# Attention stage of a fused layer: the row maxima transposed between the second gate and up products, and the residual rows' statistics given places of their own behind row maxima

## The chip, the cores and the metric

The kernel runs on one core of a Trainium2 chip. Its time is that of one execution of the whole program on the device, in microseconds (us); lower is better. The engines are TensorE (PE, with its weight loads as PEld), VectorE (DVE), ScalarE (ACT), GpSimd (POOL) and SyncE (SP), which here only issues transfers. Each works through its own list of instructions in order and waits on semaphores.

## The reference

The input x has 16 sequences of 512 rows of 256 numbers. Cut to its frame, with the two branches named:

```python
x = L0_attn_x                       # (16, 512, 256)
xn = _layernorm(x, axis=-1)
x = x + _L0_attn_ref(xn, ...) + _L0_ffn_ref(xn, ...)
# _L0_attn_ref: a state-space block (convolution, softplus, scan over 512 steps)
# _L0_ffn_ref:
y = mla(rmsnorm(xn, w_ln1), ...)    # 16 heads, causal softmax, latent keys and values
x = xn + y
x = x + moe(rmsnorm(x, w_ln2), ...) # a shared expert, and 2 of 7 experts chosen per row
```

## The kernel before

Three stages follow one another: the attention stage (`build_attn`), a stage for the chosen experts, and the state-space stage. The change is in the first alone.

The attention stage is a software pipeline over the 16 sequences. One **round** works on several sequences at once: on an older one it finishes the output projection, the second norm, the routing and the shared expert; on the next one the second pass of scores, the softmax and the values; on a younger one the first pass of scores, from which only the row maxima are kept; and on the youngest the projections. What stands where in a round is written by hand. The second pass of scores gives 64 numbered places; the table `AT` hangs every other item on a place, as (place, kind, i, j). `ORDER` is the list that results, and **every engine walks the same list** and does its own part of each item, so the table sets the order on all five engines together.

The items that matter here, with the lines of the kernel before:

- `wo` (PE L924): the output projection, four items at places 25, 27, 29 and 31. With every second one DVE adds the residual rows (L697, `f_xn<-f_Z,f_xn`), and in the kernel before also takes the statistics of those rows (L701 and L705). With the last one POOL makes from the statistics the scale of the second norm (L520 to L523) and then the sum `xs` (L526), which releases the semaphore `xs_ready`.
- `s1`: the first pass of scores (PE L840, hidden part L857, bank pair `f_Y`) and its row maxima (DVE L632). An item with j below 2 fills both banks of `f_Y`, and the next one can only start when these are read.
- `xrload`, `keep`, `stack`, `so`, `sl`: transfers on SP's queue, in this order. `xrload` (L364) waits for `xs_ready`. `keep` (L377) stores the parts of keys and queries, the six `stack` items (L387, two transfers each) read them back, `so` (L395) stores the sums of the softmax after the third `stack` item, and `sl` (L398) reads them back behind the sixth.
- `rp` (DVE L680), at place 48: the reciprocal of these sums. Behind it on DVE stand the first up product's multiplication (`u`, L770), the splitting of the maxima into three parts (`nm`, L684 to L692), the routing (`rank`, 16 small operations, L724 to L742) and the second gate product's multiplication (`g`, L766), and then the second up product's (L770).
- `nmt` (PE L903): the transposition of the split maxima, which ACT copies and SP puts beside the queries for the next round's second pass. `pfx` (PE L951, L953): the prefix sums for the routing.
- `g` and `u` (PE L960): the gate and up products of the shared expert, two each.

All of these but `s1` and the second pass share one pair of banks, `f_Z`, which are filled in turn. A product can start only when the one two before it in this ring has been read:

```python
    def freed(k, r):
        i, n = place(k, r)
        return ring_free[ring_of(k)][i], n
```

In the kernel before the order in the ring is gate 1, up 1, gate 2, up 2, `nmt`, `pfx`. So `nmt` goes into the bank of gate 2.

Of the kernel before, what the change touches and what calls it, by code (L numbers as in the profile page):

```python
# [16 lines left out]
def build_attn(nc, ctx, x_tm, out_tm, info_dram, run_dram, stat_dram, hs, w_ln1, w_ln2, W_kvd, W_qd, W_ka, W_kra, W_krb, W_qa, W_qb, W_vu, W_o,  # L17
# [7 lines left out]
    TT = SEQ // P  # L25
# [10 lines left out]
    def sb(name, shape, dt=f32):  # L36
        return ctx.enter_context(nc.sbuf_tensor(name, shape, dt))
# [38 lines left out]
    xn = sb("f_xn", [P, TT, DM])  # L76
# [15 lines left out]
    nm = sb("f_nm", [P, TT, NH])  # L92
# [8 lines left out]
    h2 = sb("f_h2", [P, TT, DM])  # L101
# [4 lines left out]
    lg = sb("f_lg", [P, TT, ER])  # L106
# [4 lines left out]
    rank = sb("f_rank", [P, TT, ER])  # L111
# [24 lines left out]
    for q in range(NG * TT):  # L136
        g, kb = divmod(q, TT)
# [7 lines left out]
    STAGE = {kind: 2 for kind in ("bnc", "h1", "h1a", "T", "lat", "kq", "split", "mid", "keep", "stack")}  # L145
    STAGE.update({kind: 1 for kind in ("stack1", "s1", "nm", "nmt", "v")})
    STAGE.update({kind: 0 for kind in ("mvx", "mvs", "xrload", "xn", "s2", "pv", "oc", "so", "sl", "rp", "ro", "rl", "ym")})
    STAGE.update({kind: -1 for kind in ("sl1", "rp1", "ro1", "rl1", "ym1", "wo", "h2", "h2a", "ht", "route", "lg", "rank", "pfx", "g", "u", "d")})
    STAGE.update({"scat": -2, "d": -2, "xload": 3, "bn": 3})
    S1 = [("s1", i, n) for i in range(NH // 2) for n in range(3)]  # L150
    AT = {}
    for n, kind, i, j in ((0, "mvx", 0, 0), (0, "bnc", 0, 0), (0, "sl1", 1, 0), (1, "stack1", 1, 0), (2, "stack1", 1, 1), (3, "stack1", 1, 2), (5, "stack1", 1, 3), (6, "stack1", 1, 4), (8, "stack1", 1, 5), (3, "d", 0, 0), (3, "h1", 0, 0), (4, "mvs", 0, 0), (5, "d", 1, 0), (5, "h1a", 0, 0),
# [4 lines left out]
                          (36, "stack", 0, 0), (37, "stack", 0, 1), (39, "stack", 0, 2), (40, "stack", 0, 3), (42, "stack", 0, 4), (43, "stack", 0, 5), (38, "ht", 0, 0), (39, "ht", 1, 0), (42, "route", 0, 0), (43, "route", 1, 0), (44, "lg", 0, 0),  # L157
                          (46, "g", 0, 0), (48, "xn", 0, 0), (49, "u", 0, 0), (50, "nm", 0, 0), (52, "rank", 0, 0), (52, "g", 1, 0), (55, "u", 1, 0),
                          (56, "nmt", 0, 0), (58, "pfx", 0, 0), (59, "bn", 0, 0)):
        AT.setdefault(n, []).append((kind, i, j))  # L160
    for n, item in enumerate(S1):
        AT.setdefault(2 + n * 47 // len(S1), []).append(item)
# [18 lines left out]
    def ring_of(k):  # L181
        return {"s2": "X", "s1": "Y"}.get(k[0], "Z")
# [16 lines left out]
    def place(k, r):  # L199

        ring = ring_of(k)
        n = index(r)
        if isinstance(n, int):
            n = sum(len(NUMBERS[m, ring]) for m in range(FIRST, n)) + NUMBERS[n, ring][k]
            return n % 2, n // 2
        first = sum(len(NUMBERS[m, ring]) for m in range(FIRST, FULL))
        n = first + (r[1] - FULL) * len(NUMBERS[FULL, ring]) + NUMBERS[FULL, ring][k]
        return n % 2, r[0] * len(NUMBERS[FULL, ring]) + n // 2
# [72 lines left out]
    def used(k, r):  # L281

        i, n = place(k, r)
        return ring_free[ring_of(k)][i], n + 1
# [4 lines left out]
    def free_sem(k, r):  # L289
        return ring_free[ring_of(k)][place(k, r)[0]]  # L290
# [136 lines left out]
    def _(pool):  # L427
# [32 lines left out]
        def chain(s, K, b, n, ins):  # L460
            ins.then_inc(s, 1)
            pool.wait_ge(s, K * b + n)

        def do(kind, i, j, b, r):
# [23 lines left out]
            if kind == "kq" and i == 1 and j % 2 == 1:  # L488
                g, n = i, j // 2
# [5 lines left out]
            if kind == "split":  # L495
                g = i
# [9 lines left out]
            if kind == "mid":  # L506
                g = i
# [5 lines left out]
            if kind in ("ym", "ym1"):  # L513
                pool.wait_ge(shares_loaded, 16 * (PAIRS * b + i + 1))
                yT = yT_[:, parity(kind, r), :, :]
                tt(yT[:, 2 * i:2 * i + 2, :], yT[:, 2 * i:2 * i + 2, :], shares[:, :, :], ALU.mult).then_inc(y_done, 1)  # L516
            if kind == "wo" and i == TT - 1:

                pool.wait_ge(stats2_done, TT * (b + 1))
                chain(sc2_step, 4, b, 1, tt(sc2[:, 0, :], mv2[:, :, 0], mv2[:, :, 0], ALU.mult))  # L520
                chain(sc2_step, 4, b, 2, tt(sc2[:, 1, :], sc2[:, 0, :], mv2[:, :, 1], ALU.add))
                chain(sc2_step, 4, b, 3, tt(sc2[:, 2, :], sc2[:, 1, :], consts[:, 1, :], ALU.pow))
                tt(sc2[:, 3, :], sc2[:, 2, :], consts[:, 2, :], ALU.add).then_inc(sc2_step, 1)  # L523
                pool.wait_ge(xr_loaded, 16 * (b + 1))
                pool.wait_ge(ot_stored, 16 * b)
                tt(xs[:, :, :], x2[:, :, :], xr[:, :, :], ALU.add).then_inc(xs_ready, 1)  # L526
            if kind == "scat":
# [4 lines left out]
                for t in range(2 * i, 2 * i + 2):  # L532
                    for k in range(TOPK):
                        pool.indirect_dma_start(hs, bass.IndirectOffsetOnAxis(ap=info_i[:, t, k:k + 1], axis=0),
                                                h2[:, t, :], None).then_inc(scattered, 16)
        run(nc.gpsimd, do)
        pool.wait_ge(scattered, 16 * TT * TOPK * BATCH)

# [86 lines left out]
    def _(dve):  # L625
        def full(k, r):
            dve.wait_ge(*filled(k, r))
            return bank_of(k, r)

        def do(kind, i, j, b, r):  # L630
# [23 lines left out]
            if kind == "kq" and i == 1:  # L654
                n = j // 2
# [37 lines left out]
            if kind == "wo" and i % 2 == 1:  # L693
                n = i // 2
                if n == 0:
                    dve.wait_ge(xn_done, 2 * b + 2)
                dve.tensor_tensor(x2[:, 2 * n:2 * n + 2, :], full(("wo", n), r)[:, :].rearrange("p (j d) -> p j d", j=2),  # L697
                                  xn[:, 2 * n:2 * n + 2, :], ALU.add).then_inc(free_sem(("wo", n), r), 1)
                for t in range(2 * n, 2 * n + 2):
                    dve.wait_ge(*used(("wo", n), r))  # L700
                    dve.bn_stats(st2[:, t, :], x2[:, t, :]).then_inc(stat2, 1)  # L701
                for t in range(2 * n, 2 * n + 2):
                    dve.wait_ge(stat2, TT * b + t + 1)
                    dve.sem_inc(taken)
                    dve.bn_aggr(mv2[:, t, :], st2[:, t, :]).then_inc(stats2_done, 1)  # L705
# [65 lines left out]
            if kind == "d":  # L771
                bank = full(("d", i), r)
                dve.wait_ge(xs_ready, b + 1)
                dve.scalar_tensor_tensor(xs[:, 2 * i:2 * i + 2, :], bank[:, :].rearrange("p (j d) -> p j d", j=2), 0.5,
                                         xs[:, 2 * i:2 * i + 2, :], ALU.mult, ALU.add).then_inc(free_sem(("d", i), r), 1)
        run(nc.vector, do)

    @block.tensor
# [1291 lines left out]
```

## Time and profile before

| | |
|---|---|
| time, median of 3 runs | 4051.83 us (4046.68 to 4064.09) |
| the profiled execution | 4053.83 us, its span 4052.0 us |
| PE busy | 88% of the span |
| DVE, ACT, POOL busy | 71%, 62%, 53% |
| attention rounds with everything in them | 78 to 85 us each, from 160 to 1290 us |
| mean granted clock of TensorE | 0.949 of full speed |

The profile is of one execution. Its timeline gives, for each engine, the start and the duration of an instruction or of a run of like ones, and in brackets how long the engine had stood idle before it and what ended that. A place in a round is found by its operation and tile: the residual addition, for instance, is the DVE row L697.

### The profile page before, as it was taken

The numbers are of one execution on the slowest core, as the hardware profiler recorded it, in microseconds if no ns is written. First come the engines' busy times: TensorE is split into PE (matmuls) and PEld (weight loads), VectorE is DVE, ScalarE is ACT, GpSimd is POOL, SyncE is SP. The second block draws the span as 40 slices with busy tenths as digits, with TensorE's granted clock in tenths as the row PEclk, the third lists the DMA queues.
The fourth block names the chain that finished last, engine by engine and source line by source line (L and its number), as shares of the span: only waits on it lengthen the run. The fifth ranks groups of instructions, "written<-read, shape, count | busy, mean of one in ns | idle before, by whom it ended". The sixth has DMA issues, their size and how long they took to land.

```text
span 4052.0 us, 70010 instructions
## 1 busy us (share of the span) xinstructions
PE 3579.4 (88%) x22072; PEld 2713.9 (67%) x22072; DVE 2892.4 (71%) x5392; ACT 2521.9 (62%) x6537; POOL 2154.4 (53%) x1083
## 2 busy tenths in 40 slices
PE   4899999999998759998799999998999999999887
PEld 1354445445554447777588888888887888888776
DVE  3455655555554222222799999999999999999997
ACT  2545555455454213332788878788887878888783
POOL 3243344334332200000578787787878778787774
PEclk7899999999999779999899999999999999999998
DMA  4333333333332167665222222121222212222221
GB/s 112 97 93 114 101 117 98 110 106 112 94 111 74 34 182 211 208 210 176 87 73 103 84 81 99 65 99 71 104 84 81 98 66 99 71 104 84 81 80 40
DMA packets 286364, 416.64 MB, mean 103 GB/s; under 512 B 78261, under 2 KB 250678, under 8 KB 263672
## 3 DMA queue, kind: packets, MB, share of 16 engines
q1 hardware_dynamic: 273048, 380.79, 29.6%
q0 software_dynamic: 12288, 33.57, 2.3%
q8 instruction: 102, 1.67, 0.2%
q10 hardware_dynamic: 864, 0.10, 0.1%
q14 instruction: 62, 0.51, 0.0%
HBM read 330.30 MB, written 83.17 MB: 102 GB/s over the span
## 4 chain that ended last, share of the span: by engine, by line
DVE 36%; issue 11%; PE 2%; POOL 1%; DVEq 1%; ACT 1%; DMA 0%; SPq 0%; POOLq 0%; ACTq 0%
DVE m_S L1774 8%; DVE m_PR L1774 8%; DVE m_S L1766 8%; DVE m_PR L1766 8%; DVE m_ub L1751 2%; DVE m_yz L1785 1%; DVE m_x L1735 1%; POOL m_ub L1554 1%; DVEq L1765 1%; DVE m_th_x L1743 1%; ACT m_dA L1663 1%; PE m_F L1884 0%; PE m_Y L1922 0%; PE m_F L1858 0%; PE m_F L1934 0%
## 5 line engine op out<-in xcount | busy, mean ns | idle before, releaser
L1554 POOL TENSOR_TENSOR m_ub<-m_Bb,m_dtx 128x2048 f32<-128x2048 f32 x254 | 1157.0, 4567 | 280.6 <-PE m_Y L1922 176.1
L1663 ACT ACTIVATE m_dA<-m_dt,m_a_neg 128x128 f32<-128x128 f32 x4096 | 1211.1, 388 | 129.6 <-DVE m_S L1774 129.2
L1922 PE MATMUL m_Y<-m_ub,m_ident 128*128 128x128 f32 x8192 | 956.2, 278 | 62.7 <-DVE m_ub L1751 62.4
L1922 PEld LDWEIGHTS m_Y<-m_ub,m_ident 128*128 128x128 f32 x8192 | 939.5, 194 | 73.8 <-DVE m_ub L1751 73.5
L632 DVE TENSOR_REDUCE f_nm<-f_Y 128x1 f32<-128x512 f32 (+3 forms) x896 | 432.4, 531 | 308.9 <-PE f_Y L857 306.8
L552 ACT ACTIVATE f_pt<-f_X 128x512 f32<-128x512 f32 (+1 forms) x704 | 372.5, 556 | 406.8 <-PE f_X L857 403.5
L1766 DVE SCALAR_TENSOR_TENSOR m_PR<-m_dA,m_S 128x512 f32<-128x512 f32 x512 | 355.8, 695 | 26.1 <-POOL m_ub L1554 7.5
L1766 DVE SCALAR_TENSOR_TENSOR m_S<-m_dA,m_PR 128x512 f32<-128x512 f32 x512 | 354.8, 693 | 12.0
L1774 DVE CUSTOM_DVE_ANT_1 m_S<-m_S,m_ub 128x512 f32<-128x512 f32 x512 | 353.2, 690 | 0.8 <-issue 0.8
L1774 DVE CUSTOM_DVE_ANT_1 m_PR<-m_PR,m_ub 128x512 f32<-128x512 f32 x512 | 353.2, 690 | 0.2 <-DVE m_PR L1766 0.2
L1751 DVE TENSOR_TENSOR m_ub<-m_S,m_Cb 128x512 f32<-128x512 f32 x512 | 349.5, 683 | 0.0
L1751 DVE TENSOR_TENSOR m_ub<-m_PR,m_Cb 128x512 f32<-128x512 f32 x512 | 349.3, 682 | 0.0
L516 POOL TENSOR_TENSOR f_yT<-f_yT,f_shares 128x1024 f32<-128x1024 f32 x32 | 75.3, 2353 | 462.3 <-DMA f_shares<-f_shares_dram 462.3
L1884 PE MATMUL m_F<-m_xpad,m_cv_diag 128*128 128x256 f32 x1024 | 285.6, 427 | 0.0
L840 PE MATMUL f_Y<-f_kst,f_qst 96*128 96x512 bf16 (+3 forms) x1024 | 236.8, 316 | 52.0 <-DVE f_nm L632 27.6
L1200 DVE SCALAR_TENSOR_TENSOR e_sg<-e_th,e_G 128x512 f32<-128x512 f32 x70 | 48.1, 687 | 324.7 <-ACT e_th L1144 324.7
L846 PE MATMUL f_X<-f_qst,f_kst 99*128 99x512 bf16 (+3 forms) x1024 | 253.6, 317 | 27.3 <-ACT f_pt L552 19.2
L1505 POOL MEMSET m_ident<- 128x128 f32 x1 | 0.2, 205 | 470.2 <-POOLq L2047 470.2
L1884 PEld LDWEIGHTS m_F<-m_xpad,m_cv_diag 128*128 128x128 f32 x1024 | 201.5, 207 | 71.4 <-issue 45.2
L1858 PE MATMUL m_F<-m_xnT,m_w_in 128*128 128x256 f32 x1024 | 236.0, 384 | 2.6 <-DMA m_w_in<-L_attn_W_in 1.6
L840 PEld LDWEIGHTS f_Y<-f_kst,f_qst 96*128 96x128 bf16 x1024 | 88.3, 102 | 186.2 <-issue 87.3
L1858 PEld LDWEIGHTS m_F<-m_xnT,m_w_in 128*128 128x128 f32 x1024 | 193.1, 193 | 28.1 <-DMA m_w_in<-L_attn_W_in 2.0
(233 smaller groups left out, 6009.6 us busy)
## 6 DMA issues: line engine op xcount, KB each, us to landing
m_Bb<-m_bc_dram SPq DMA_DIRECT2D x64, 1024.0 KB, 4.7
m_Cb<-m_bc_dram SPq DMA_DIRECT2D x64, 1024.0 KB, 6.3
f_parts_dram<-f_parts SPq DMA_DIRECT2D x32, 768.0 KB, 4.1
f_kst<-f_parts_dram SPq DMA_DIRECT2D x192, 128.0 KB, 2.6
f_qst<-f_parts_dram SPq DMA_DIRECT2D x192, 128.0 KB, 2.6
e_rows<-sorted_rows SPq DMA_DIRECT2D x70, 256.0 KB, 2.8
e_wg<-Wg SPq DMA_DIRECT2D x70, 256.0 KB, 2.9
e_wu<-Wu SPq DMA_DIRECT2D x70, 256.0 KB, 4.0
```

Source lines behind the costliest of these rows:

```text
L552: act.activation(out, cols(bank_of(k, r)), func, **kw).then_inc(free_sem(k, r), 1)
L632: ins = dve.tensor_reduce(out, cols(full(k, r)), AX.X, ALU.max, negate=True)
L840: pe.matmul(bank[:, c0:c0 + n], qst[p][0:KS, h, qb * P:(qb + 1) * P], kst[p][0:KS, h, 0:n], start=(c0 == 0), stop=False, skip_group_check= ...
L846: pe.matmul(bank[:, c0:c0 + n], kst[p][:, h, kb * P:(kb + 1) * P], qst[p][:, h, kb * P:SEQ], start=(c0 == 0), stop=False, skip_group_check ...
L1554: pool.tensor_tensor(ub[:, h, i, :, :], Bb[:, s, :, :], dtx[:, m, None, s * SN:(s + 1) * SN].to_broadcast([P, NST, SN]), ALU.mult).then_in ...
L1663: last = act.activation(dA[:, h, i, n, :], dtt[:, par, m, s * SN:(s + 1) * SN], ACT.Exp, scale=a_neg[:, m, n:n + 1])
L1751: return dve.tensor_tensor(ub[:, h, 1:3, :, cols], state[:, :].rearrange("p (i n b) -> p i n b", i=2, n=NST), Cb[:, s, None, :, cols].to_b ...
L1766: dve.scalar_tensor_tensor(new, dA[:, h, :, :, cols].rearrange("p i n b -> p (i n) b"), DA_MIN, old, ALU.max, ALU.mult).then_inc(p_step, 1)
L1774: dve._custom_dve(bass.dve_ops.TENSOR_ADD_SAT, out=new, in0=new, in1=ub[:, h, 0:2, :, cols].rearrange("p i n b -> p (i n) b"), s0=CLIP, s1 ...
L1858: last = pe.matmul(F[(1 + i) % 4][:, m, :], w_in[:, k, blk * P:(blk + 1) * P], xnT[:, k, :], start=(k == 0), stop=(k == KM - 1))
L1884: last = pe.matmul(F[1 + i][:, j, :], cv_diag[:, k * MI + m, :], xpad[:, m, k * BATCH:k * BATCH + CN], start=False, stop=(k == TAPS - 1))
L1922: last = pe.matmul(Y[:, i * SN:(i + 1) * SN], ident[:, :], ub[:, h, 1 + i, n, :], start=False, stop=(n == NST - 1), skip_group_check=True)
```

## The change

Two things are moved. First, the statistics of the residual rows become an item of their own, `x2s`, at places 28 and 32, one place behind the residual addition, and POOL's chain on them goes with the second one. The reciprocal and the scaling of the second norm (`h2`, `h2a`) move one place down. Second, `nmt` moves from place 56 to 54, the second up product from 55 to 57, and `pfx` from 58 to 59. No instruction is added or taken away.

```diff
@@ -145,7 +145,7 @@
-    STAGE.update({kind: -1 for kind in (..., "wo", "h2", ...)})
+    STAGE.update({kind: -1 for kind in (..., "wo", "x2s", "h2", ...)})
...
@@ -153,10 +153,10 @@
-                          (29, "wo", 2, 0), (30, "mid", 1, 0), (31, "wo", 3, 0), (33, "xrload", 0, 0), (34, "keep", 1, 0), (34, "h2", 0, 0), (35, "h2a", 0, 0),
+                          (28, "x2s", 0, 0), (29, "wo", 2, 0), (30, "mid", 1, 0), (31, "wo", 3, 0), (32, "x2s", 1, 0), (33, "xrload", 0, 0), (34, "keep", 1, 0), (35, "h2", 0, 0), (36, "h2a", 0, 0),
...
-                          (46, "g", 0, 0), (48, "xn", 0, 0), (49, "u", 0, 0), (50, "nm", 0, 0), (52, "rank", 0, 0), (52, "g", 1, 0), (55, "u", 1, 0),
-                          (56, "nmt", 0, 0), (58, "pfx", 0, 0), (59, "bn", 0, 0)):
+                          (46, "g", 0, 0), (48, "xn", 0, 0), (49, "u", 0, 0), (50, "nm", 0, 0), (52, "rank", 0, 0), (52, "g", 1, 0),
+                          (54, "nmt", 0, 0), (57, "u", 1, 0), (59, "pfx", 0, 0), (59, "bn", 0, 0)):
@@ -514,7 +514,7 @@
-            if kind == "wo" and i == TT - 1:
+            if kind == "x2s" and i == 1:
 
                 pool.wait_ge(stats2_done, TT * (b + 1))
@@ -696,6 +696,8 @@
                 dve.tensor_tensor(x2[:, 2 * n:2 * n + 2, :], full(("wo", n), r)[:, :].rearrange("p (j d) -> p j d", j=2),
                                   xn[:, 2 * n:2 * n + 2, :], ALU.add).then_inc(free_sem(("wo", n), r), 1)
+            if kind == "x2s":
+                n = i
                 for t in range(2 * n, 2 * n + 2):
                     dve.wait_ge(*used(("wo", n), r))
                     dve.bn_stats(st2[:, t, :], x2[:, t, :]).then_inc(stat2, 1)
```

From L698 on, a line of the kernel before has a number higher by two in the changed one.

**DVE, at the second pair of residual rows.** `f_xn<-f_Z,f_xn` is the residual addition, `f_st` and `f_mv` are the statistics, `f_nm<-f_Y` are row maxima, three operations for one head of `s1`. Before:

```order
L697 TENSOR_TENSOR f_xn<-f_Z,f_xn 128x512
L701 BN_STATS f_st<-f_xn 128x6 x2
L705 BN_AGGR f_mv<-f_st 128x2 x2
L632 TENSOR_REDUCE f_nm<-f_Y 128x1 x6
L708 RECIPROCAL f_sc<-f_sc 128x4
L632 TENSOR_REDUCE f_nm<-f_Y 128x2
```

The changed kernel, at the same place:

```order
L697 TENSOR_TENSOR f_xn<-f_Z,f_xn 128x512
L632 TENSOR_REDUCE f_nm<-f_Y 128x1 x3
L703 BN_STATS f_st<-f_xn 128x6 x2
L707 BN_AGGR f_mv<-f_st 128x2 x2
L632 TENSOR_REDUCE f_nm<-f_Y 128x1 x3
L710 RECIPROCAL f_sc<-f_sc 128x4
L632 TENSOR_REDUCE f_nm<-f_Y 128x2
```

Three row maxima of one head now stand ahead of the statistics.

**PE, at the second gate and up products.** `f_Z<-f_h2T,f_wg` is a gate product, `f_Z<-f_h2T,f_wu` an up product, `f_Z<-f_identb,f_nm_part` is `nmt`, `f_X` is the second pass of scores, `f_O` the values, and `f_Z<-f_chosen,f_tri` the start of `pfx`. The list is read from the second gate product on; what only repeats is left to the rows shown. Before:

```order
L873 MATMUL f_O<-f_pt,f_va 32x512 x4
L784 REGISTER_ALU
L960 MATMUL f_Z<-f_h2T,f_wu 128x512 x2
L846 MATMUL f_X<-f_qst,f_kst 128x384
L857 MATMUL f_X<-f_mask_k,f_identb 128x128
L900 REGISTER_ALU
L903 MATMUL f_Z<-f_identb,f_nm_part 48x128 x4
L784 REGISTER_ALU
L846 MATMUL f_X<-f_qst,f_kst 128x384
L857 MATMUL f_X<-f_mask_k,f_identb 128x128
L846 MATMUL f_X<-f_qst,f_kst 128x256 x2
```

The changed kernel, at the same place:

```order
L875 MATMUL f_O<-f_pt,f_va 32x512 x4
L786 REGISTER_ALU
L902 REGISTER_ALU
L905 MATMUL f_Z<-f_identb,f_nm_part 48x128 x4
L848 MATMUL f_X<-f_qst,f_kst 128x384
L859 MATMUL f_X<-f_mask_k,f_identb 128x128
L786 REGISTER_ALU
L848 MATMUL f_X<-f_qst,f_kst 128x384
L859 MATMUL f_X<-f_mask_k,f_identb 128x128
L962 MATMUL f_Z<-f_h2T,f_wu 128x512 x2
L848 MATMUL f_X<-f_qst,f_kst 128x256 x2
```

`nmt` and the second up product have changed places around two items of the second pass. In the ring of banks the order becomes gate 1, up 1, gate 2, `nmt`, up 2, `pfx`: `nmt` goes into the bank of up 1, and up 2 into that of gate 2.

## Rows read from the trace of the kernel before

**Rows 1.** The page: busy time of TensorE and its share of the span.

```profile
PE 3579.4 (88%) x22072; PEld 2713.9 (67%) x22072; DVE 2892.4 (71%) x5392; ACT 2521.9 (62%) x6537; POOL 2154.4 (53%) x1083
```

**Rows 2.** Waits, 170 to 1300 us: total us, times, longest.

```profile
DVE f_sums L680 <- DMA f_sums<-f_sums_dram: 38.1, 13, 5.0
...
PE f_Z L903 <- DVE f_sg L766: 32.3, 14, 4.0
```

**Rows 3.** Timeline (start, us, operation), PE: second up product, `nmt`; last row another round.

```profile
565.11 1.99 PE L960 MATMUL f_Z<-f_h2T,f_wu 128*128 128x512 f32 x4
566.93 0.33 PE L846 MATMUL f_X<-f_qst,f_kst 99*128 99x384 bf16 x1
...
570.75 0.38 PE L903 MATMUL f_Z<-f_identb,f_nm_part 128*48 128x128 bf16 x4 [3.44 <-DVE f_sg L766]
...
974.08 0.38 PE L903 MATMUL f_Z<-f_identb,f_nm_part 128*48 128x128 bf16 x4 [0.74 <-DVE f_sg L766]
```

**Rows 4.** Timeline, DVE, from the reciprocal of the sums to the second gate.

```profile
563.50 0.35 DVE L680 RECIPROCAL f_sums<-f_sums 128x32 f32<-128x32 f32 x1 [3.86 <-DMA f_sums<-f_sums_dram]
...
565.28 0.20 DVE L692 CAST f_nm_part<-f_nm_rest 128x64 bf16<-128x64 f32 x1
...
569.83 0.68 DVE L766 SCALAR_TENSOR_TENSOR f_sg<-f_th,f_Z 128x512 f32<-128x512 f32 x1
```

**Rows 5.** Timeline, SP's queue: when it issued.

```profile
546.65 0.38 SPq L364 DMA_DIRECT2D f_xr<-x_tm  x1
547.42 0.37 SPq L377 DMA_DIRECT2D f_parts_dram<-f_parts  x1
553.11 0.53 SPq L387 DMA_DIRECT2D f_kst<-f_parts_dram  x1
...
561.41 0.43 SPq L398 DMA_DIRECT2D f_sums<-f_sums_dram  x1
```

**Rows 6.** Timeline, POOL: the chain on the statistics and the sum `xs`.

```profile
542.15 0.20 POOL L520 TENSOR_TENSOR f_sc<-f_mv 128x4 f32<-128x4 f32 x1 [2.87 <-DVE f_mv L705]
...
543.99 2.35 POOL L526 TENSOR_TENSOR f_xs<-f_xn,f_xr 128x1024 f32<-128x1024 f32 x1
```

**Rows 7.** Timeline, DVE, behind the last output projection; the last row is of another round.

```profile
540.27 0.69 DVE L697 TENSOR_TENSOR f_xn<-f_Z,f_xn 128x512 f32<-128x512 f32 x1 [2.04 <-PE f_Z L924]
540.99 0.75 DVE L701 BATCH_NORM_STATS2 f_st<-f_xn 128x6 f32<-128x256 f32 x2
...
541.99 2.67 DVE L632 TENSOR_REDUCE f_nm<-f_Y 128x1 f32<-128x512 f32 x6
...
943.61 0.69 DVE L697 TENSOR_TENSOR f_xn<-f_Z,f_xn 128x512 f32<-128x512 f32 x1 [2.04 <-PE f_Z L924]
```

**Rows 8.** Timeline, PE, behind the last output projection.

```profile
542.71 0.39 PE L840 MATMUL f_Y<-f_kst,f_qst 96*128 96x512 bf16 x1 [1.24 <-DVE f_nm L632]
...
543.37 0.39 PE L840 MATMUL f_Y<-f_kst,f_qst 96*128 96x384 bf16 x2 [0.21 <-DVE f_nm L632]
```

**Rows 9.** Timeline, PE, from `nmt` to the values' projection, in a round at full clock.

```profile
651.46 0.38 PE L903 MATMUL f_Z<-f_identb,f_nm_part 128*48 128x128 bf16 x4 [2.13 <-DVE f_sg L766]
651.77 0.34 PE L846 MATMUL f_X<-f_qst,f_kst 99*128 99x384 bf16 x1
...
652.01 0.38 PE L846 MATMUL f_X<-f_qst,f_kst 99*128 99x256 bf16 x2
...
652.90 0.39 PE L846 MATMUL f_X<-f_qst,f_kst 99*128 99x256 bf16 x2 [0.29 <-ACT f_pt L552]
...
655.83 0.91 PE L834 MATMUL f_Z<-f_w_q,f_lat 64*128 64x256 f32 x3
```

**Rows 10.** Windows: stretch, length, busy time of PE, PEld, DVE, ACT, POOL; granted clock.

```profile
570.70:575.70 5.00, 4.66 (x38) 1.97 (x38) 3.36 (x16) 2.24 (x5) 2.36 (x1) 0.66 0.14 47
651.40:656.40 5.00, 4.47 (x49) 2.36 (x50) 3.77 (x15) 3.07 (x6) 1.68 (x1) 1.00 0.18 58
...
711.00:716.00 5.00, 5.00 (x34) 2.41 (x37) 1.93 (x5) 1.42 (x3) 0.00 (x0) 0.66 0.27 85
```

More of the change, by code:

```diff
@@ L147, in build_attn @@
     STAGE.update({kind: 0 for kind in ("mvx", "mvs", "xrload", "xn", "s2", "pv", "oc", "so", "sl", "rp", "ro", "rl", "ym")})
-    STAGE.update({kind: -1 for kind in ("sl1", "rp1", "ro1", "rl1", "ym1", "wo", "h2", "h2a", "ht", "route", "lg", "rank", "pfx", "g", "u", "d")})
+    STAGE.update({kind: -1 for kind in ("sl1", "rp1", "ro1", "rl1", "ym1", "wo", "x2s", "h2", "h2a", "ht", "route", "lg", "rank", "pfx", "g", "u", "d")})
     STAGE.update({"scat": -2, "d": -2, "xload": 3, "bn": 3})
```

## The prediction, made before the changed kernel was run

> **What bounds the kernel now.** I first read the page. TensorE is busy 88% of the whole span [rows 1], and only the attention stage is changed, so the question is which waits of TensorE in a round are real. The chain that ended last is no help here, since it follows the last stage. So I went to the waits of the stretch in which full rounds run. Two rows matter [rows 2]: `nmt` on TensorE waits for the second gate product's multiplication on DVE 14 times, 2.3 us each on average and up to 4.0 us, and DVE waits 13 times for the sums of the softmax to come back from memory. The timelines of one round show that the second wait makes the first. I call the moment at which `nmt` may start T. In the round shown T is 570.75 us [rows 3].
>
> Followed back from T, the round shows these links. The gate multiplication starts at 569.83, at the end of a run of DVE work without a gap that began at 563.50 with the reciprocal of the sums [rows 4]. That reciprocal waited 3.86 us for the sums. Their load was issued at 561.41, behind the twelve `stack` transfers that began at 553.11, and these waited for the store of the parts, issued at 547.42 [rows 5]. That store stands on SP's queue behind `xrload`, issued at 546.65, which waits for `xs`. POOL ends `xs` at 543.99 + 2.35 = 546.34, and began its chain at 542.15, after the statistics [rows 6]. The statistics start at 540.99, right behind the residual addition at 540.27 [rows 7]. Not one link has slack: **from the residual addition to T it is one chain**, 570.75 - 540.27 = 30.48 us. In another round it is 974.08 - 943.61 = 30.47 us, although there TensorE waited only 0.74 us and not 3.44 [rows 3, 7]. A chain that is equally long whatever TensorE does beside it sets the time. TensorE's own work between its two ends is covered by it, and what TensorE does behind T, up to the next residual addition, is dense. So a round is as long as that chain, plus TensorE's work behind T.
>
> **The change, part by part.** No instruction is added, so everything is a matter of places.
>
> *Row maxima ahead of the statistics, first pair of rows (place 28).* The POOL chain waits for the second pair anyway. I cost this at nothing; what covers it is the 6 us until the second pair is there. Without that cover it would be the same 1.2 us as in the next item.
>
> *The same, second pair (place 32).* Six maxima take 2.67 us [rows 7], so three take 1.33. They start right at the addition's end, some 0.6 us after its start, where the statistics now start 0.72 after it. So the statistics are later by 0.6 + 1.33 - 0.72 = 1.2 us, and so is every link up to T. The bounds are 0, if a slower thing took over on SP's queue, and 1.33, if the maxima hide nothing. In the row SP issues `xrload` 0.31 us after `xs` ends, with nothing in between, so I take the 1.2. It holds in 13 rounds, those in which DVE waits for the sums [rows 2]: 13 x 1.2 = **15.6 us**.
>
> What this buys is on TensorE. The next head's first pass now waits 1.24 us for a bank, and another 0.21 [rows 8], since the maxima stand behind the statistics. They will be free about 1.1 us sooner. But this lies inside the chain's 30.5 us, so TensorE only comes sooner to the wait at T. I cost it at nothing. It would be worth up to 1.45 x 13 = 18.9 us if TensorE and not the chain were the bound there. The reciprocal for the second norm and its scaling on ACT also come about 1 us later, because POOL's chain ends later. Three maxima stand behind the reciprocal on DVE; that delay too lies inside the chain.
>
> *`nmt` ahead of the second up product.* `nmt` now needs up 1's bank and the split maxima, which end at 565.28 + 0.20 [rows 4], later by the 1.2. TensorE reaches it at about 565.1, where the up product starts today [rows 3], and waits about a microsecond. Its ACT copy and its transfers, queued behind it, are early then; the second pass that needs them never waited for them in a full round, so this gives nothing there.
>
> *The second up product behind T.* It needs the bank of gate 2, whose multiplication stands on DVE behind the whole routing, as before. So the wait at T does not go; **it moves from `nmt` to the up product**. Today the up product runs ahead of T, from 565.11 to 566.93, 1.82 us [rows 3], under cover of the chain. Now it runs behind it. What goes ahead of T in exchange is `nmt`, 651.77 - 651.46 = 0.31 us, and an item of the second pass, 652.01 - 651.77 = 0.24; and the wait of 0.29 for an exponential of ACT shortly behind it should go as well, because ACT has caught up [rows 9]. That leaves 1.82 - 0.84 = 1.0 us. The bounds are 0.8 (if the other short wait for ACT, of 0.18, goes too) and 1.3 (if both stay). 14 rounds have this wait: 14 x 1.0 = **14 us**.
>
> *The clock.* The 5 us behind T ran at a granted clock of 0.66 in the round shown and at 1.00 in another [rows 10]; of the 14 rounds, eight were low there and six were not. Low is the level of 1.2 GHz for a part of the window: 5 x (1 - 0.66) = 1.7 us lost. TensorE now stands idle for longer in front of T. At the least no further round falls, at the most six do: 0 to 6 x 1.7 = 10.2 us. I take two, **3.4 us**, because the clock also fell in a stretch in which TensorE had been fully busy (711 to 716 [rows 10]), so that idle time is not all that decides it.
>
> The Trainium skill ("TensorE: Matmul & The Clock Gate", section "Why this matters for your kernels") warns that an idle gap between bursts of matmuls brings the clock back to its lower level. By that rule every one of the 14 rounds would restart low, and the term would be 10.2 us and not 3.4. The 711 row does not follow from it.
>
> *Sum.* 15.6 + 14 + 3.4 = 33 us. Against the profiled execution's own 4053.83 us that is 4087; this execution lies 2 us above the median of the three runs, so I say **4085 us**, 0.8% slower. Runs of this kernel differ by a few microseconds, up to 17 between the fastest and slowest shown, and a difference below 0.5%, some 20 us, can't be told from none.
>
> **The rivals.**
>
> 1. *Only the up product counts; the statistics' delay is lost.* If the transfer that stores the parts, or SP's issue of `stack`, is limited by something else, 1.2 us of later `xs` vanish. For it: from the issue at 547.42 to 553.11 the store takes 5.7 us, and that may vary. Against it: the equal 30.48 and 30.47. Time 4051.8 + 14 = 4066. Chance 0.13.
>
> 2. *No effect that can be measured.* The up product behind T fills time in which TensorE would wait for ACT, and the shift is lost as in 1. Against it: only 0.29 + 0.18 us of such waits are in the rows behind T. Time 4052. Chance 0.09.
>
> 3. *Faster: TensorE is the bound.* The place is the first pass behind the last output projection. Its waits of 1.24 and 0.21 us go in 13 rounds: 4052 - 19 = 4033 us. For this to count, T must come before TensorE reaches the second up product. Today TensorE waits 2.3 us for T on average, and in the new order reaches its waiting item 1.3 us earlier still (1.82 less the 0.55 that goes ahead). So it decides only once the chain is shorter by more than about 3.6 us, and nothing in the change shortens it. Chance 0.11, for what I overlook.
>
> 4. *The clock falls in all rounds.* The rows then give 15.6 + 14 + 10.2 = 40, or with the up product itself at half speed in these six rounds (another 1.8 us each) up to 51: 4092 to 4103 us. For it: two idle stretches of TensorE in place of one, and the second long. Against it: the clock fell without idle time too. It is the rule of the skill named above, as a mechanism of this kernel. Chance 0.10.
>
> My forecast, both terms with few further falls of the clock, has the chance that is left, 0.57, with a range of its own from 4074 to 4092.
>
> **How the numbers follow.** Slower by more than 0.5% (above 4072) are the forecast and rival 4, 0.57 + 0.10 = 0.67. Within 0.5% are rivals 1 and 2, 0.22. Faster is rival 3, 0.11. The range for 8 in 10 takes in the forecast, rivals 1 and 4 and the upper half of rival 2: 4052 to 4101. Outside are rival 3, the other half of rival 2 and the tip of rival 4, about 0.17.
>
> **What the profile of the changed kernel would show.** On TensorE: `nmt` (L905) with a wait of about 1 us that ends by the split of the maxima; the second up product (L962) with a wait of 3 to 6 us that ends by the gate multiplication on DVE (L768); the first pass behind the last output projection with almost no wait. From the residual addition to T 31.7 us in place of 30.5; from T to the values' projection 5.4 us in place of 4.4 at full clock; the full rounds about 2.3 us longer. The prediction is wrong if the chain keeps its 30.5 us (the first term is then gone), if the up product doesn't wait for the gate's multiplication (the second), or if rounds get shorter, which would mean that TensorE's own work was the bound.

## The result and the profile after

The changed kernel takes 4087.26 us in the median of six runs (4083.69 to 4091.79), the kernel before 4050.98 us on the same chip (six runs, 4046.68 to 4068.84). The ratio is 1.0075, with a 95% interval from 1.0057 to 1.0093. The medians lie 36 us apart; by the ratio the change makes the kernel slower by 30 us, with an interval from 23 to 38. 4085 us had been forecast.

The page of the changed kernel: the span, and the busy time of the engines.

```profile
span 4087.8 us, 70010 instructions
...
PE 3573.9 (87%) x22072; PEld 2714.1 (66%) x22072; DVE 2883.9 (71%) x5392; ACT 2522.0 (62%) x6537; POOL 2152.5 (53%) x1083
```

The engines do the same work as before [rows 1]; the span has grown by waiting. Where, the waits between 170 and 1300 us show (engine, line and tile; what it waited for; total us, times, longest):

```profile
DVE f_sums L680 <- DMA f_sums<-f_sums_dram: 59.3, 13, 5.2
...
PE f_Z L962 <- DVE f_sg L768: 51.8, 13, 4.1
...
PE f_Z L905 <- DVE f_nm_part L692: 14.8, 11, 1.7
```

Before, `nmt` waited 32.3 us for the gate's multiplication and DVE 38.1 us for the sums [rows 2]. Now it is the second up product that waits, 51.8 us, and `nmt` has a short wait of its own for the split of the maxima.

The timeline of one round shows the chain again. DVE, from the residual addition on:

```profile
624.84 0.69 DVE L697 TENSOR_TENSOR f_xn<-f_Z,f_xn 128x512 f32<-128x512 f32 x1 [2.04 <-PE f_Z L926]
625.45 1.34 DVE L632 TENSOR_REDUCE f_nm<-f_Y 128x1 f32<-128x512 f32 x3
626.71 0.74 DVE L703 BATCH_NORM_STATS2 f_st<-f_xn 128x6 f32<-128x256 f32 x2
```

POOL, at the sum `xs`:

```profile
629.70 2.36 POOL L526 TENSOR_TENSOR f_xs<-f_xn,f_xr 128x1024 f32<-128x1024 f32 x1
```

SP's queue:

```profile
632.37 0.38 SPq L364 DMA_DIRECT2D f_xr<-x_tm  x1
633.14 0.37 SPq L377 DMA_DIRECT2D f_parts_dram<-f_parts  x1
639.02 0.52 SPq L387 DMA_DIRECT2D f_kst<-f_parts_dram  x1
...
647.35 0.43 SPq L398 DMA_DIRECT2D f_sums<-f_sums_dram  x1
```

DVE, at the other end of the chain:

```profile
649.26 0.35 DVE L680 RECIPROCAL f_sums<-f_sums 128x32 f32<-128x32 f32 x1 [4.84 <-DMA f_sums<-f_sums_dram]
...
655.59 0.68 DVE L768 SCALAR_TENSOR_TENSOR f_sg<-f_th,f_Z 128x512 f32<-128x512 f32 x1
```

The statistics start 626.71 - 624.84 = 1.87 us after the addition, against 0.72 [rows 7]. Every link up to the store of the parts is later by the same 1.15 us: the store is issued 8.30 us after the addition, against 547.42 - 540.27 = 7.15 [rows 5, 7]. TensorE in the same round:

```profile
626.19 0.39 PE L842 MATMUL f_Y<-f_kst,f_qst 96*128 96x512 bf16 x1
...
651.38 0.38 PE L905 MATMUL f_Z<-f_identb,f_nm_part 128*48 128x128 bf16 x4 [1.44 <-DVE f_nm_part L692]
...
656.32 3.64 PE L962 MATMUL f_Z<-f_h2T,f_wu 128*128 128x512 f32 x4 [4.00 <-DVE f_sg L768]
...
663.16 1.13 PE L836 MATMUL f_Z<-f_w_q,f_lat 64*128 64x256 f32 x4
```

The first pass at 626.19 has lost its wait of 1.24 us [rows 8], and nothing came of it. The up product stands behind the wait, and its row is 3.64 us long, against 1.99 before [rows 3], since the clock is down. The windows of 5 us from the end of the wait on (length, busy time of PE, PEld, DVE, ACT and POOL, granted clock):

```profile
242.70:247.70 5.00, 4.96 (x20) 2.35 (x23) 0.90 (x3) 0.62 (x2) 0.97 (x1) 0.60 0.13 47
...
656.30:661.30 5.00, 4.98 (x23) 2.24 (x23) 0.94 (x3) 0.92 (x2) 2.13 (x1) 0.66 0.11 44
...
821.00:826.00 5.00, 4.91 (x11) 2.28 (x12) 0.73 (x2) 0.39 (x1) 1.27 (x1) 0.50 0.15 54
...
1310.90:1315.90 5.00, 5.00 (x23) 2.22 (x23) 1.16 (x4) 1.16 (x2) 2.35 (x1) 0.66 0.09 29
```

All 14 rounds are low there, between 0.50 and 0.69. Before, eight were [rows 10]. In the 13 rounds with a long wait the clock falls 1.6 to 4.4 us before the wait ends, and is still low when the up product starts. In the round shown TensorE stands idle from 652.32 to 656.32:

```profile
651.90:652.80 0.90, 0.41 (x4) 0.13 (x2) 0.83 (x3) 0.90 (x3) 0.00 (x0) 1.00 0.10 18
653.00:656.00 3.00, 0.00 (x0) 0.00 (x0) 2.65 (x12) 0.62 (x2) 0.00 (x0) 0.50 0.31 105
```

**Where the time went.** I read each round's residual addition, the end of the wait (T) and the start of the values' projection (L834, L836 after) from the timelines, and took means over the 13 rounds in a row:

| us per round | before | after | difference |
|---|---|---|---|
| residual addition to T | 31.07 | 31.54 | +0.47 |
| T to the values' projection | 5.34 | 7.22 | +1.88 |
| values' projection to the next addition | 43.99 | 43.70 | -0.29 |
| whole round | 80.41 | 82.46 | +2.05 |

The third row is not an effect of the change that I can name: 3.6 and 1.6 us of it come from two rounds that were long before, 1.4 the other way from a third, and the ten others differ by 0.12 us at most. Over 13 rounds the whole is 26.7 us. The expert stage's first gate multiplication starts at 1487.5 us and not at 1461.6, 25.9 later. The remaining 10 of the spans' 35.8 us lie in the two later stages, most of it, 7.7 us, between that row and the start of the scan's sums (514.4 before, 522.1 after). The change doesn't touch this stage, and it took between 514.5 and 521.1 us in the eight profiles of the first and the third group below, so I count that part as scatter between executions.

### The profile page after: what moved, and what is told of

It reads as the page before. It is cut to its first block, busy times and chain, and to the rows that moved or that the text cites. A ratio compares the mean times of both kernels' runs of the same rounds, so it can differ in the third digit from the quotient of the medians.

```text
span 4087.8 us, 70010 instructions
## 1 busy us (share of the span) xinstructions
PE 3573.9 (87%) x22072; PEld 2714.1 (66%) x22072; DVE 2883.9 (71%) x5392; ACT 2522.0 (62%) x6537; POOL 2152.5 (53%) x1083
## 4 chain that ended last, share of the span: by engine, by line
DVE 36%; issue 11%; PE 2%; ACT 1%; DVEq 1%; POOL 1%; DMA 0%; SPq 0%; POOLq 0%; ACTq 0%
DVE m_S L1776 8%; DVE m_PR L1776 8%; DVE m_S L1768 8%; DVE m_PR L1768 8%; DVE m_ub L1753 2%; DVE m_yz L1787 1%; ACT m_dA L1665 1%; DVE m_x L1737 1%; DVEq L1767 1%; DVE m_th_x L1745 1%; PE m_Y L1924 1%; PE m_F L1886 1%; POOL m_ub L1556 0%; PE m_F L1860 0%; PE m_F L1884 0%
```

## The experiments

All ratios are to the kernel before on the same chip in the same group, with 95% intervals. The kernels ran in three groups of four, each group on a chip of its own. The kernel before took 4056.89 us on the first, 4177.02 on the second (e5 to e8) and 4055.11 on the third, so kernels are set against each other within a group, and across groups only by their ratios.

**One half alone: the products.**

```diff
--- before
+++ e1_nmt_only
-(52, "rank", 0, 0), (52, "g", 1, 0), (55, "u", 1, 0), (56, "nmt", 0, 0), (58, "pfx", 0, 0),
+(52, "rank", 0, 0), (52, "g", 1, 0), (54, "nmt", 0, 0), (57, "u", 1, 0), (59, "pfx", 0, 0),
```

> Kernel before, with only the transposition, the second up product and the prefix sums moved (places 54, 57, 59); the statistics stay where they were. Chain theory: residual addition to the end of the second gate's multiplication keeps the length of the kernel before (31.1 us in the mean, statistics starting 0.72 us after the addition), the second up product waits about 3 us for that multiplication, and from there to the values' projection it takes about 7.2 us, as in the changed kernel, in place of 5.3: about 25 us slower than before, 4076 us. If the delay of the statistics were the larger part of the loss: 10 us slower at most, 4061 us.

Measured 1.0046 (1.0032 to 1.0059): 18.7 us slower on 4056.89. The statistics start 0.72 us after the addition again, and T comes at 30.70 us in the mean. From T to the values' projection it takes 6.76 us (5.34 before). This half costs about what the prediction had for it with the clock, 14 + 3.4, and less than the 25 us expected of this run, since the clock behind T was low in 11 of the 14 rounds and not in all. Two rounds with about the same wait, 3.19 and 3.07 us, differ in it:

```profile
569.30:574.30 5.00, 4.82 (x44) 2.29 (x44) 2.60 (x4) 1.68 (x3) 2.36 (x1) 1.00 0.10 39
...
1056.80:1061.80 5.00, 4.96 (x13) 2.33 (x14) 0.69 (x1) 0.44 (x1) 2.35 (x1) 0.50 0.09 38
```

**The other half alone: the statistics.**

```diff
--- after
+++ e2_stats_only
-(52, "rank", 0, 0), (52, "g", 1, 0), (54, "nmt", 0, 0), (57, "u", 1, 0), (59, "pfx", 0, 0),
+(52, "rank", 0, 0), (52, "g", 1, 0), (55, "u", 1, 0), (56, "nmt", 0, 0), (58, "pfx", 0, 0),
```

> Changed kernel, with the transposition, second up product and prefix sums put back to places 56, 55 and 58; only the statistics are moved. Chain theory: statistics start 1.87 us after the addition in place of 0.72, every link to the transposition is 1.15 us later, 0.5 to 1.15 us of it left in the mean; behind the wait 5.3 us as before: 6 to 15 us slower than before, 4057 to 4066 us. If TensorE's own work bounds that part of the round: the two waits for a bank of row maxima (1.24 and 0.21 us) go and it is up to 19 us faster, 4032 us.

Measured 1.0031 (1.0021 to 1.0040): 12.6 us slower, within the first theory's 6 to 15. T comes at 31.65 us and not 31.07, and behind it the round takes 6.02 us and not 5.34, since TensorE now waits up to 4.1 us for T and the clock is low behind it in 13 of 14 rounds; 5.3 had been expected there. So more than half of what this half costs is clock, 0.68 us a round against 0.58 ahead of T. The rival, that TensorE's own work is the bound there and rounds get shorter, is out. The two halves add up to 0.77%; the whole is 0.75%.

**The gate's multiplication ahead of the routing, in the kernel before.**

```diff
--- before
+++ e3_gate_before_rank
-(52, "rank", 0, 0), (52, "g", 1, 0)
+(52, "g", 1, 0), (52, "rank", 0, 0)
```

> Kernel before, with one swap: at place 52 the second gate product's multiplication stands ahead of the routing on DVE. Chain theory: the gate's bank comes free about 4.5 us sooner (right behind the split of the maxima), which is 26 us after the residual addition, before TensorE gets to the transposition in most rounds; the wait of 2.3 us in the mean goes in 14 rounds, with it the falls of the clock behind it: 32 to 45 us faster, 4006 to 4019 us. The prefix sums then wait up to 1 us for the routing: 14 us back at most. If TensorE's wait was only a symptom, and other work fills its place: same as before.

Measured 1.0064 (1.0045 to 1.0083), slower. I missed this one. `nmt` lost its wait, as expected, but another wait took its place a few rows on. TensorE in one round:

```profile
647.55 0.40 PE L903 MATMUL f_Z<-f_identb,f_nm_part 128*48 128x128 bf16 x4
...
652.03 0.17 PE L951 MATMUL f_Z<-f_chosen,f_tri 128*128 128x28 bf16 x1 [3.26 <-DVE f_sg L770]
```

and DVE beside it:

```profile
650.92 0.21 DVE L742 TENSOR_REDUCE f_info<-f_picked 128x8 f32<-128x56 f32 x1
651.09 0.69 DVE L770 TENSOR_TENSOR f_sg<-f_sg,f_Z 128x512 f32<-128x512 f32 x1
```

In the ring of banks the prefix sums come two behind the second up product, whose multiplication still stands behind the routing. I had looked only at the values that the prefix sums need, which were there at 649.3, and not at their bank. Between 170 and 1300 us this wait adds up to a little more than `nmt`'s 32.3 us before:

```profile
PE f_Z L951 <- DVE f_sg L770: 35.7, 14, 3.3
```

That explains why nothing was won, but not the 26 us lost: the profiled execution is the fastest of the six (4068.8 us), and its 13 rounds took 80.70 us and not 80.41. What differs in all executions is the clock. Its mean was 0.940 to 0.945 in the six and 0.946 to 0.950 in those of the kernel before, which is 233 us lost against 210 ((1 - clock) x span, in the mean), nearly the whole difference. Why more falls come with this order was not tested.

**The store of the parts first on SP's queue, in the kernel before.**

```diff
--- before
+++ e4_keep_before_xrload
-(33, "xrload", 0, 0), (34, "keep", 1, 0)
+(33, "keep", 1, 0), (34, "xrload", 0, 0)
```

> Kernel before, with one swap on SP's queue: the second store of the parts is issued ahead of the load of the residual's rows, so it no longer waits for xs. Chain theory: the store is issued up to 8 us sooner (its data are ready at about 539.3 in the round shown), so the sums are back before DVE asks for them; DVE's wait of 2.9 us goes in 13 rounds, and the transposition then waits only for DVE's own work: 25 to 38 us faster, 4013 to 4026 us. If the link from xs to the store was not what set the chain (another thing holds SP's queue or DVE): same as before.

Measured 0.9938 (0.9925 to 0.9952), 25 us faster, at the weak end of what was expected. This takes out one link of the chain, and the link was real. The run was repeated beside others, below, and its rows stand there.

**The gate's multiplication ahead of the routing, in the changed kernel.** The edit is that of e3, on the changed kernel.

> Changed kernel, with the second gate product's multiplication ahead of the routing on DVE (as in the run before that tried this on the kernel before). There the prefix sums waited for the bank of the second up product, whose multiplication stands behind the routing; here they have the bank of the transposition. So nothing on TensorE but the prefix sums depends on the routing. Theory of the chain: the second up product runs without a long wait at about 27.5 us after the residual addition, the prefix sums wait 0.5 us or so, the values' projection comes at 33.5 us in place of 38.4: about 60 us faster than the changed kernel and 38 faster than before, 4019 us. If another wait takes the place again, as in that run: 4060 to 4085 us.

Measured 0.9878 (0.9857 to 0.9899). Here the swap helps, by about 2% if set against the changed kernel's 1.0075, though that was not measured on this chip. The second up product has no wait any more, and the values' projection comes 32.65 us after the addition and not 38.76. So the same swap costs 0.64% in one order of products and helps in the other. The prefix sums now stand in the bank of `nmt`, and their wait for the up product's multiplication (the row of L951 above) is gone. The clock differs too: 0.942 to 0.946 here against 0.936 to 0.941 for the kernel before on this chip.

**The store first, in the changed kernel.** The edit is that of e4, on the changed kernel.

> Changed kernel, with the store of the parts ahead of the load of the residual's rows on SP's queue. The chain from the statistics is cut, so their delay should cost nothing; what is left of the change's loss is the second up product behind the wait. Theory: 1.0 us a round (14 us) slower than the kernel before with the same swap on SP's queue (4035 us there), which is 4049 us; if the clock falls behind the wait in every round as in the changed kernel, up to 27 us more than it, 4062 us. If the order of TensorE's products were not a cause at all: 4035 us or less.

Measured 0.9918 (0.9899 to 0.9936). This is the run that shows the price of the order of TensorE's products by itself, against e8 below, which differs from it in that order alone: 0.9918 against 0.9882, 0.36% of 4177 or 15 us, where 14 had been expected. The size is rough: the medians lie 13 us apart, the six times of each spread over 17 and 18 us, and the two intervals overlap. A part is clock, which was low behind T in four rounds of e6 and in none of e8. A round of it in which the clock stayed up:

```profile
767.36 1.98 PE L962 MATMUL f_Z<-f_h2T,f_wu 128*128 128x512 f32 x4 [1.61 <-DVE f_sg L768]
...
772.20 0.42 PE L875 MATMUL f_O<-f_pt,f_va 128*32 128x128 f32 x8 [0.18 <-ACT f_pt L552]
772.55 0.70 PE L836 MATMUL f_Z<-f_w_q,f_lat 64*128 64x256 f32 x2
```

From T to the values' projection 5.19 us, against 4.37 [rows 9]: 0.8 us a round, the lower bound of the prediction. The wait of 0.29 us for ACT is gone, that of 0.18 is not.

**Both swaps in the changed kernel.**

> Changed kernel, with both swaps: the gate's multiplication ahead of the routing, and the store of the parts ahead of the load of the residual's rows. Theory: nothing is left of the chain in front of the second gate, TensorE's own work is the bound, and the places of the change (maxima ahead of the statistics, transposition ahead of the up product) now pay: rounds of about 76.5 us in place of 80.4, 50 us faster than before, 4005 us. If TensorE then waits for the routing before the prefix sums by as much as is saved: 4020 to 4035 us.

Measured 0.9875 (0.9852 to 0.9898), 52 us faster, as large as expected. The absolute times can't be set against the expectation's, since on this chip a part of the rounds stands still for some microseconds on several engines at once behind the values' projection. One such stretch, in e5, on DVE:

```profile
964.83 0.69 DVE L632 TENSOR_REDUCE f_nm<-f_Y 128x1 f32<-128x512 f32 x1 [7.12 <-remote]
```

**Statistics moved, store first, products as before.** The edit of e4 on e2.

> Kernel before with the statistics moved as in the change, and the store of the parts first on SP's queue; the order of TensorE's products is that of the kernel before. Compared with the kernel before with SP's swap alone (4035 us): if the delay of the statistics cost only by the chain through SP's queue, this is not slower than that, and if TensorE is the bound now, the waits of 1.24 and 0.21 us that go are worth up to 19 us: 4020 to 4035 us. If the delay costs by another way (second norm, its scaling, the waits for them): 4040 us or more.

Measured 0.9882 (0.9861 to 0.9903). It is not slower than e7, and far from the 0.9938 of e4 on the first chip. Whether that is the statistics' doing or the chip's, only one chip could tell.

**Four kernels on one chip.** The last group repeats e4, the changed kernel, e8 and e7 side by side.

> The kernel before with the store of the parts first on SP's queue, once more, beside the next three on one chip, since the chips of the two earlier calls differ by 3% on the kernel before and only runs of one call can be set against each other. Expected 0.6% faster than the kernel before, as on the other chip, if the chip only adds a constant; nearer to 1% if it does not.

Measured 0.9939 (0.9923 to 0.9954). The waits between 170 and 1300 us have no row any more for DVE and the sums, and `nmt`'s is

```profile
PE f_Z L903 <- DVE f_sg L766: 7.0, 14, 0.5
```

0.5 us a round and not 2.3. SP's queue in one round, whose residual addition is at 599.77 us:

```profile
606.16 0.38 SPq L364 DMA_DIRECT2D f_xr<-x_tm  x1
606.95 0.54 SPq L387 DMA_DIRECT2D f_kst<-f_parts_dram  x1
```

The reading back of the parts is issued right behind `xrload`, 7.2 us after the addition and not 12.8, because the store has long landed. T comes at 29.88 us in the mean (31.07 before), and from there to the values' projection it takes 4.39 us in the mean and never more than 4.44, without a fall of the clock.

> The changed kernel once more, in the same call. Expected 0.75% slower than the kernel before, as measured first. Chain theory: with the two halves of the change at 0.46% and 0.31%, the sum is 0.77%.

Measured 1.0075 (1.0058 to 1.0093), the same as the first time. So are the rounds: 31.49 us to T and 7.28 from there to the values' projection.

> The kernel before with the statistics moved and the store of the parts first, once more. This tells whether the maxima ahead of the statistics pay when the chain through SP's queue is cut: against the same kernel without moved statistics (in this call) up to 19 us faster if the two waits for a bank of 1.24 and 0.21 us count in full, about 8 us if half of it comes back at the next places, 0 if the second norm's delay eats it.

Measured 0.9892 (0.9872 to 0.9912). Against e9 that is 0.47% of 4055, 19 us. The size is what the two waits were worth, 1.45 x 13, but the rows do not bear out that way to it. The first pass behind the output projection in e9:

```profile
602.21 0.39 PE L840 MATMUL f_Y<-f_kst,f_qst 96*128 96x512 bf16 x1 [1.24 <-DVE f_nm L632]
```

and in e11, where the residual addition is at 600.99:

```profile
602.34 0.39 PE L842 MATMUL f_Y<-f_kst,f_qst 96*128 96x512 bf16 x1
603.00 0.39 PE L842 MATMUL f_Y<-f_kst,f_qst 96*128 96x384 bf16 x2 [0.21 <-DVE f_nm L632]
```

and two more rows of e11, further down in the same round:

```profile
604.56 0.39 PE L842 MATMUL f_Y<-f_kst,f_qst 96*128 96x256 bf16 x2 [0.51 <-DVE f_nm L632]
...
606.73 0.39 PE L842 MATMUL f_Y<-f_kst,f_qst 96*128 96x384 bf16 x2 [0.94 <-DVE f_nm L632]
```

The wait of 1.24 us is gone, but 0.51 + 0.94 = 1.45 us came back at two of the next first passes, for row maxima as before, since DVE has as much to do as before. At full clock nothing is gained: T comes 27.58 us after the addition in the one round of e9 without a fall of the clock, and 27.65 to 27.77 in eight rounds of e11. The difference is the clock. In e9 all but one of the 13 rounds had a fall between the addition and T, most of them two, and with two T came at about 30.27 us; in e11 eight of 13 had none, and the mean is 28.32 and not 29.88. That is the 1.6 us by which the round of e11 is shorter, 76.60 and not 78.18. It is no accident of the two profiled executions: the mean clock was 0.955 to 0.957 in all four executions of e11 and 0.949 to 0.952 in all six of e9. **The same places of the statistics cost 12.6 us with the chain through SP's queue, and give 19 us without it, by way of the clock.** Why three short waits bring fewer falls than one of 1.24 us and one of 0.21 was not tested.

> The changed kernel with both swaps (gate's multiplication ahead of the routing, store of the parts first), once more. In the call before it was 1.25% faster than the kernel before and 0.07% faster than the run of moved statistics and store first, less than can be told. Expected the same here: the order of the second up product then brings nothing of its own, since the up product's multiplication behind the routing is waited for by the values' projection.

Measured 0.9886 (0.9866 to 0.9906), not to be told from e11, as expected; so the changed kernel with both swaps is about 1.9% faster than the changed kernel as it stands, on one chip. The values' projection comes 1.0 us sooner than in e11 (31.66 against 32.70), but 0.75 of it is lost again up to the next addition. A part is a new wait in the second half of that projection, for the bank of the prefix sums:

```profile
640.77 1.13 PE L836 MATMUL f_Z<-f_w_q,f_lat 64*128 64x256 f32 x4 [0.30 <-DVEq L758]
```

The waits between 170 and 1300 us count eight of them, 4.6 us in all and 1.1 the longest; three others, 4.5 us in all, are for the up product's multiplication. The rest I did not trace.

## Why the prediction was right, point by point

**The chain.** Shown. e4 and e9 cut one link of it, SP's wait for `xs` ahead of the store, and 25 us went, with DVE's wait for the sums. The statistics' delay of 1.2 us a round measured 1.15, and it reached the issue of the store undiminished. But of the term's 15.6 us only 13 x 0.47 = 6 us arrived at T, in the mean. The store took 5.83 us from its issue to the first reading back, in the mean, against 6.11 before; with the moved statistics of e2 and e10 it was 5.79 and 5.81, in e1 and e3 without them 5.94 and 6.10. So one term's size was off: the transfer behind the delay gave about a quarter of it back. All of this quarter comes from three rounds of the trace before, in which the store took 6.9 to 7.2 us; its ten others took 5.6 to 6.1, the 13 of the changed kernel 5.6 to 6.0. Why the slow stores stay away when the store starts later is open. Another 0.2 us a round is chance: in one round of the trace before, POOL's chain was 2.6 us late, as DVE had waited for its own next instruction. The last 0.2 lies between the first reading back and T, 17.65 us before and 17.46 after. The prediction took the chain's 30.5 us from two rounds; both are among the short ones of the 13 (30.3 to 33.3 us, 31.07 in the mean), which it could not see from them. The store's own time, 5.6 to 7.2 us, is a link that varies.

**The second up product behind T.** The wait moved from `nmt` to the up product, as said. At full clock its price is 5.19 - 4.39 = 0.8 us a round and not 1.0 (e6): 14 x 0.8 = 11 us and not 14. The lower bound came true for another reason than the one given: the short wait of 0.18 us for ACT still stands. What was saved beside the 0.29 are 0.16 us at the prefix sums and the two items of the second pass beside them, which take 0.87 us from 769.18 to 770.05 and took 1.32 from 652.01 to 653.33, the 0.29 included.

**The clock.** This step failed in size. I took two further falls, 3.4 us; all 14 rounds fell. From T to the values' projection it is now 7.20 us over the 14 rounds against 5.19 at full clock, 2.0 lost, where 5.28 against 4.39, 0.9, were lost before: 14 x 1.1 = 15 us. That is what rival 4 had said of the falls, and what the rule of the Trainium skill said ("TensorE: Matmul & The Clock Gate", section "Why this matters for your kernels"); for the 13 waits of 3.8 to 4.1 us the trace agrees with it. It does not hold for every gap: after waits of 3.1 and 3.2 us the clock stayed at 1.00 in two rounds of e1. Its price stayed below the 10.2 + 11 us allowed there. Both halves of the change have a share in it: 14 x 0.57 = 8 us in e1 and 14 x 0.63 = 9 in e2, so the statistics cost more by the clock behind T than by delaying T. Nor is it a matter of more falls in all. The mean clock was 0.946 to 0.951 in the six executions of e10 and in the 11 of the kernel before beside them. What changed is where the clock is low: behind T and no longer under the cover of the chain. The forecast total was right by luck, because the first term was too large and the third too small by nearly the same amount: 6 + 11 + 15 - 4 (the third row of the table) = 28 us, of the 29 by which the last values' projection lies further from the first addition in the trace, against 33 forecast. The -4 is the scatter of three rounds named above.

**The row maxima's gain, costed at nothing.** Right, and more so than I had argued: even with the chain cut, the wait that goes comes back as 1.45 us further down, which I had not seen (e11). The 19 us of e11 over e9 have the size of rival 3's price, but not its mechanism; they are falls of the clock that stayed away. Under the chain of the kernel before and of the changed one such falls, between the addition and T, are covered.

**Rivals 1 and 2** said that the delay is lost or that nothing can be measured. e2 excludes both: the statistics alone cost 0.31%, with an interval that doesn't reach 0.2%.

**`nmt`'s own wait.** A microsecond was said; it was 1.44 in the round shown, and the waits count 11 of them, 1.3 us in the mean.

## What to carry to other kernels

Before moving an operation off an engine's path, follow what it releases: here three row maxima ahead of two small statistics took a wait of 1.24 us from TensorE and put 1.15 us on SP's queue, where a load waited for the statistics and a store that others needed stood behind it. With the store first the same move turned from a loss into a gain.

Where products share a ring of banks, count each one's bank two places back on both engines. The same swap on DVE cost 0.64% in one order and helped in the other. In the first the prefix sums waited 3.26 us for a bank, in the second they did not; the clock differed too, and how much each counts was not separated.

Work that is put behind a wait loses its cover, and may run at the lower clock on top. Here, with both halves of the change, the second cost more than the first, about 15 us against 11; with the order of the products alone about 8 against 11.

## What the runs showed of the hardware

The granted clock of TensorE behind a wait. In the changed kernel it was low behind T in all 14 rounds (0.50 to 0.69 over 5 us), 13 of them after waits of 3.8 to 4.1 us and the last after 1.61; in e9, after 0.5 us, in none of the 14. In between both occurred: in e1 after 3.1 to 3.2 us (rows above), in the last round of e10 the clock stayed up after 1.60 us, and after the same wait of some 1.6 us two rounds of e6 read

```profile
328.20:333.20 5.00, 4.97 (x23) 2.20 (x23) 0.90 (x3) 0.87 (x2) 2.34 (x1) 0.66 0.07 21
...
767.30:772.30 5.00, 4.76 (x40) 2.23 (x44) 2.49 (x5) 1.68 (x3) 2.37 (x1) 1.00 0.09 29
```

Elsewhere the falls kept a place in the round that no long wait explains. In nine rounds of e4 in a row the clock was low some 4 us and again some 14 us behind the residual addition, 1.7 us of full clock lost each time, with no wait of TensorE near the first but the 1.24 and 0.21 us, and near the second but one of 0.23. In e11 and e12, without that wait, 22 and 25 us were lost between 200 and 1320 us, against 52 in e4 and 49 in e9. What sets these falls stays open.

The times differ by chip. The kernel before took 4177 us on one and 4055 to 4057 us on the two others, and in the four kernels traced on the slow one the rounds' part from the values' projection to the next addition took 52 to 54 us and not 44, with waits on several engines at once while GpSimd issued its scattered stores. Each chip was used for one group only, so whether this belongs to the chip can't be told. Even so, the ratios of e7 and of its repetition e12 agree, 0.9875 and 0.9886, as do those of e8 and e11, 0.9882 and 0.9892.
